# Output products of eight experts with both halves of the second weight in one 512 column operand, the halves added by VectorE, and a new order around them

## The reference

```python
h = gelu(einsum('ecd,edh->ech', buf, w1) + b1[:, None, :])      # 640 x 256 by 256 x 1024
out = einsum('ech,ehd->ecd', h, w2) + b2[:, None, :]            # 640 x 1024 by 1024 x 256
y = einsum('ned,ne->nd', gathered, weights)                     # by gate, summed over experts
x = layernorm(x + y)
```

## Time and profile before

| | |
|---|---|
| median of 3 runs | 974.79 us |
| the profiled execution | 970.69 us, of which the span from first to last instruction is 968.9 us |
| PE busy, share of span | 911.5 us, 94% |
| ACT, DVE, POOL busy | 728.8, 602.7, 455.0 us |
| mean granted TensorE clock | 0.984 |
| experts' part | from 699.9 us to the end at 968.9 us |
| hidden stages (L1518) | 768 products of 320 columns, 116.7 us busy |
| output stages (L1537) | 960 products of 256 columns, 123.8 us busy |

### The profile page before, as it was taken

How to read it: one execution, slowest core, us unless ns; L and a number is a source line. 1 busy time by engine, 2 the same in 40 slices (tenths; PEclk the granted TensorE clock), 3 DMA queues, 4 the chain that set the end, 5 groups by cost and what they waited for, 6 DMA issues and landing times. The chain is left out here.

```text
span 968.9 us, 19742 instructions
## 1 busy us (share of the span) xinstructions
PE 911.5 (94%) x7569; PEld 513.2 (53%) x7569; DVE 602.7 (62%) x1162; ACT 728.8 (75%) x889; POOL 455.0 (47%) x382
## 2 busy tenths in 40 slices
PE   8799999999989999998999999998599999999995
PEld 6333343344333334333433433344599999989994
DVE  5666446547785555787555767347457676667675
ACT  6588878887777888787789789985265678567863
POOL 0265225144355634546464435423525455654574
PEclk9899999999999999999999999999799999999998
DMA  7759442333534335344342327231365434543311
GB/s 219 233 202 353 142 166 70 122 142 132 189 133 159 117 120 186 137 161 136 139 158 100 135 97 239 98 102 35 99 231 164 137 112 135 181 135 108 124 60 61
DMA packets 62201, 139.75 MB, mean 144 GB/s; under 512 B 10242, under 2 KB 31299, under 8 KB 61584
## 3 DMA queue, kind: packets, MB, share of 16 engines
q1 hardware_dynamic: 41040, 74.46, 24.0%
q0 software_dynamic: 21056, 63.93, 18.5%
HBM read 71.43 MB, written 66.54 MB: 142 GB/s over the span
## 5 line engine op out<-in xcount | busy, mean ns | idle before, releaser
L689 ACT ACTIVATE prob<-spsum 128x1024 f32<-128x1024 f32 x512 | 493.1, 1021 | 111.3 <-PE spsum L881 103.3
L905 PE MATMUL opsum<-prob,val 128*17 128x512 f32 x2048 | 271.3, 599 | 1.3 <-DVE oraw L1271 0.4
L881 PE MATMUL spsum<-area_q 32*128 32x512 f32 x1536 | 133.5, 429 | 5.7 <-DMA area_q<-aT 3.3
L881 PE MATMUL spsum<-stacks 32*128 32x512 f32 x1536 | 134.4, 425 | 1.6 <-ACT prob L689 1.0
L881 PEld LDWEIGHTS spsum<-area_q 32*128 32x128 f32 x1536 | 73.1, 185 | 118.5 <-ACT prob L689 63.6
L881 PEld LDWEIGHTS spsum<-stacks 32*128 32x128 f32 x1536 | 73.5, 183 | 115.5 <-ACT prob L689 63.5
L1279 DVE RECIPROCAL oden<-oden 128x256 f32<-128x256 f32 x62 | 108.7, 1753 | 2.1
L574 POOL TENSOR_TENSOR onorm<-oraw,oden 128x512 f32<-128x512 f32 x31 | 41.6, 1343 | 119.5 <-DVE oden L1279 115.1
L519 POOL TENSOR_TENSOR area_s<-emb,area_s 128x1024 fp32r<-128x1024 f32 x28 | 66.5, 2377 | 53.0 <-DVE area_s L1097 53.0
L517 POOL TENSOR_TENSOR square<-raw 128x512 bf16<-128x512 f32 x28 | 53.7, 1918 | 80.3 <-DVE raw L1077 80.2
L905 PEld LDWEIGHTS opsum<-prob,val 128*17 128x17 f32 x2048 | 36.1, 95 | 102.2 <-ACT prob L689 63.9
(11 more groups left out here) (212 smaller groups left out, 1227.1 us busy)
## 6 DMA issues: line engine op xcount, KB each, us to landing
split_scratch<-area_s POOLq DMA_DIRECT2D x60, 512.0 KB, 5.0
area_k<-in_w SPq DMA_DIRECT2D x16, 1024.0 KB, 7.4
stacks<-split_scratch SPq DMA_DIRECT2D x28, 512.0 KB, 5.5
area_q<-split_scratch SPq DMA_DIRECT2D x28, 512.0 KB
dispatched<-blank POOLq DMA_DIRECT2D x1, 5300.0 KB, 25.3
rows<-dispatched SPq DMA_DIRECT2D x7, 662.5 KB
res<-in_x SPq DMA_DIRECT2D x4, 1024.0 KB, 9.3
aT<-onorm SPq DMA_DIRECT2D x124, 32.0 KB
```

Of the source, the lines that this page charges most:

```text
L689: act.activation(prob[u % NPB][:], spsum[u % NSB][:].rearrange("p a n -> p (a n)"), ACT.Exp, scale=HD ** -0.5).then_inc(s_exp, 1)
L881: ins = pe.matmul(spsum[u % NSB][:, j % 2, :], kst[par][rows, a, P * kt:P * (kt + 1)], qst[par][rows, b, cols], start=i == 0, stop=i == 2 ...
L905: ins = pe.matmul(opsum[32 * j:32 * j + HD + 1, :], val[b % 2][:, kt, h0 + j, :], prob[(2 * s + j // 2) % NPB][:, HALF * (j % 2):HALF * (j ...
```

## The change

The order of the three products changes and their form: for each slice m one product of 512 columns takes the high half of the hidden values by both halves of w2 (`high_part`); its result fills the whole bank `yp`, the right half holding the contribution of the low half of w2. One product of 256 columns (`low_part`) adds low by high into the left half. So 16 products replace 24 in a tile, with the same count of columns. `add_own` gets a second DVE instruction that adds the right half into `others`.

PE's order in tiles 0 and 1 changes: the last slice of tile 0 comes behind half of tile 1's high products. On DVE `prepare`, `scale_and_shift` and `add_own` of tiles 0 and 1 go ahead of `turned`, and `remainder` 2 and 3 both go behind the last tile. ACT's `normalise` calls start at tile 0 and are spread over the tiles, `second_half` comes at tile 2. POOL's `store_outputs` and `gather_sums` move accordingly.

```diff
+            def high_part(e, t, first, end):
+                n = ST * e + t
+                if first == 0 and n >= 2:
+                    pe.wait_ge(s_z, n - 1)
+                for m in range(first, end):
+                    if t == 0:
+                        pe.wait_ge(s_hhi, HK * e + m + 1)
+                    pe.matmul(yp[n % 2][:].rearrange("p (s d) -> p s d", s=2),
+                              hids[:, 0, m, P * t:P * (t + 1)], w2s[e % 2][:, :, m, :],
+                              start=m == 0, stop=False)
+            def low_part(e, t, first, end):
+                n = ST * e + t
+                for m in range(first, end):
+                    if t == 0:
+                        pe.wait_ge(s_hid, HK * e + m + 1)
+                    ins = pe.matmul(yp[n % 2][:, 0:DIM], hids[:, 1, m, P * t:P * (t + 1)],
+                                    w2s[e % 2][:, 0, m, :], start=False, stop=m == HK - 1)
+                if end == HK:
+                    ins.then_inc(s_y, 1)
...
-                    if e + 1 < EXPERTS:
-                        for tt in TURNS[t]:
-                            turn(e + 1, tt)
-                    n = ST * e + t
-                    if n >= 2:
-                        pe.wait_ge(s_z, n - 1)
-                    for m in range(HK):
-                        if t == 0:
-                            pe.wait_ge(s_hid, HK * e + m + 1)
-                        for i, (a, b) in enumerate(TERMS):
-                            ins = pe.matmul(yp[n % 2][:, 0:DIM], hids[:, a, m, P * t:P * (t + 1)],
-                                            w2s[e % 2][:, b, m, :], start=m == 0 and i == 0,
-                                            stop=m == HK - 1 and i == 2)
-                    ins.then_inc(s_y, 1)
+                    if e + 1 < EXPERTS and t != 1:
+                        turn(e + 1, t)
+                    if t == 0:
+                        high_part(e, 0, 0, HK - 1)
+                        low_part(e, 0, 0, HK - 1)
+                        if e + 1 < EXPERTS:
+                            turn(e + 1, 1)
+                        high_part(e, 1, 0, HK // 2)
+                        high_part(e, 0, HK - 1, HK)
+                        low_part(e, 0, HK - 1, HK)
+                    else:
+                        high_part(e, t, HK // 2 if t == 1 else 0, HK)
+                        low_part(e, t, 0, HK)
...
                     if e + 1 < EXPERTS:
                         turned_high(e + 1, t)
-                        if t == 1:
+                        if e:
+                            normalise(e - 1, e - 1, ((0,), (1, 2), (), (3,), (4,))[t])
+                        if t == 2:
                             second_half(e + 1)
-                        if e and t >= 2:
-                            normalise(e - 1, e - 1, ((0, 1), (2, 3), (4,))[t - 2])
...
                 dve.wait_ge(s_y, n + 1)
+                link(dve.scalar_tensor_tensor(others[:, t, :], yp[n % 2][:, DIM:2 * DIM], g, others[:, t, :],
+                                              ALU.mult, ALU.add))
                 dve.scalar_tensor_tensor(eo[e % 2][:, t, :], yp[n % 2][:, 0:DIM], g, others[:, t, :],
                                          ALU.mult, ALU.add).then_inc(s_z, 1)
...
-                    if e + 1 < EXPERTS:
-                        for tt in TURNS[t]:
-                            turned(e + 1, tt)
-                        if t:
-                            remainder(e + 1, t - 1)
+                    if e + 1 < EXPERTS and t >= 2:
+                        turned(e + 1, t)
                     prepare(e, t)
...
                     add_own(e, t)
+                    if e + 1 < EXPERTS:
+                        if t < 2:
+                            turned(e + 1, t)
+                        for part in ((), (0,), (1,), (), (2, 3))[t]:
+                            remainder(e + 1, part)
```

On POOL:

```diff
-                    store_outputs(e - 2, 2)
+                    pool.wait_ge(s_h, HK * e + 2)
                     store_outputs(e - 2, 3)
...
-                    pool.wait_ge(s_h, HK * e + 2 + t)
+                    pool.wait_ge(s_h, HK * e + 3 + t)
                     gather_sums(e, t)
...
-                    if e and t >= 2:
-                        store_outputs(e - 1, t - 2)
-            for t in range(2, ST):
+                    if e and t:
+                        store_outputs(e - 1, t - 1)
+            for t in range(ST - 2, ST):
                 store_outputs(LAST - 1, t)
```

More of the change, by code:

```diff
@@ L1397, in experts @@
         block = ctx.enter_context(nc.Block())
-        TURNS = ((0,), (1,), (2,), (3,), (4,))
         @block.sync
```

## The result

The changed kernel takes 961.7 us (median of 4 runs, 961.35 to 962.78) against 974.58 of the kernel before beside it (4 runs, 972.11 to 976.84): a ratio of 0.9873, with an interval of 0.9853 to 0.9893. The gain is 12.9 us where 7.5 was forecast.

A forecast was written before the change was run, and what follows sets the result against it. Bound: the ACT and DVE chain to tile 2 in experts 1 to 6, DVE's queue in expert 7. Terms -9.8 + 1.2 - 1.1 + 2.3 - 0.1 = -7.5 took 974.8 to 967.3 us; range 962.5 to 974.0.

The forecast's parts named there:

- The bound: Experts 1 to 6: the chain through ACT and DVE, not PE, sets tile 2's start, 7.78 us behind the last gelu.
- DVE's order: Experts 1 to 6: tile 2 starts at gelu + 6.15 instead of 7.78, 9.8 us less before late stores.
- the middle that I took for late stores: Experts 2 to 6: 1.2 us given back for late output stores, between ends of 0 and 2.4.
- The store: `add_own(e, 0)` may wait for the last output store, taken to land 3.35 us after issue; 1.2 us back.
- the bounds 0 and 2.4: Lateness of stores in experts 2 to 6: 0 if POOL's moves bring them in time, 2.4 us if nothing changes.
- The products: Where PE sets the pace, 23 tiles: 231.5 ns per 512-column product, 0.05 us saved a tile, 1.1 us in all.
- Rivals C: High products of 512 columns are dearer: at 269 ns each the gain is gone, at 325 ns 992 us; chance 0.10.
- D (131 ns): High products take 131 ns by the skill page's rule, DVE then sets the pace: 961 us; chance 0.03.
- Expert 7: DVE sets the pace there: five more adds cost 2.6 us, 0.3 back for an earlier start, net 2.3 slower.
- late low parts: Sign of being wrong: remainder pieces behind the last tile delay first low parts until gelus and PE wait; no size given.

The follow-up runs named there:

- turned_later: The kernel before with one move on DVE alone, `turned(e + 1, 0)` behind `add_own(e, 0)`; 960.34 us beside 967.19, ratio 0.9914.
- order_only: The changed kernel with two products of 256 columns for each high one and a single add, new order kept; 961.95 us, ratio 0.9867.
- after_pool_old: The changed kernel with POOL's program of before for output stores, gathers and their waits; 962.77 us beside 967.19, ratio 0.9942.

## Why the forecast was too small, and what in it held

**The bound.** That the start of tile 2 was set by the chain through ACT's rounding and DVE's queue is shown: turned_later moves one instruction of it and the 7.78 become 6.25.

**DVE's order.** Forecast was tile 2 at gelu + 6.15. It is at 6.24 to 6.26 where the store is in time, and 6.6 in experts 2, 5 and 6. With the middle that I took for late stores (1.2 us in all) the term was -8.6; it measured -8.1. What is late next isn't the adds but ACT's copy and PE itself. In expert 1, where the last gelu is at 753.92, the timeline of DVE after the change has

```profile
759.42 0.42 DVE L1662 TENSOR_TENSOR xe<-tp,xe 128x256 fp32r<-128x256 f32 x1 [0.20 <-ACT xe L1585]
```

so the second add is done 0.20 us before ACT's copy, and `turned` ends at 5.92. PE's transpositions begin at 6.08, 0.06 us after tile 1. I had PE free at 5.61, counted from a first transposition 0.43 ahead of the gelu; in expert 2 that gelu was a late one, undisturbed it is 0.20, and two tiles with their transpositions take 6.2 to 6.3 us and not 6.0. turned_later and order_only have one add less and the same 6.25, with waits of 0.7 us for ACT's copy. So the second add costs nothing until a store is late.

**The store.** It is issued no earlier than in before (in expert 2 the last gelu is at 783.38 and the store at 785.30, 1.92 behind it, 1.69 before), but took 2.90 us to land, not the 3.35 I had taken or the 3.80 of the earlier trace rows. DVE waited for it in three experts by 0.4 to 0.5 each, 1.3 us in all, and tile 2 came 1.1 us later for it, close to the 1.2. That the middle came out is partly chance: turned_later has a landing of 3.83, and after_pool_old shows what a later store costs, 3.7 us at one place. I gave the moves on POOL the bounds 0 and 2.4; the upper one had left out the clock.

**The products.** Eight high products take 1.87 us, 234 ns each, and eight low ones 0.94, 117 each; the line through the earlier trace rows gave 231.5 for a high one. A tile takes 2.81 us instead of 2.85, so the saving per tile was right, 0.04 against 0.05. 18 tiles gave 0.7. Expert 0 kept its period (30.84 and 30.80), although its tiles gave 0.25: its first gelu comes 3.56 us behind the first product instead of 3.35, as 3.2 us of the stage lay at half the granted clock and not 2.7. Rivals C (269 ns or more) and D (131 ns) are both out. The Trainium skill (TensorE: Matmul & The Clock Gate, Back-to-back issue gap) has N / 2.4 + 2.5 ns for an isolated gap, 216 ns at 512 columns, and about 131 in a stream; this trace has 234, above both.

**Expert 7.** Forecast +2.3, measured +1.1. From the first add (936.37) to the last (950.60) it is 14.2 us where before had 11.2, 3.1 more. The five adds are 2.6 of it, as forecast; the rest is a wait for ACT's ln and exp in front of the second tile's adds (timeline of DVE):

```profile
939.30 0.16 DVE L1345 TENSOR_TENSOR lnt<-lnt 128x1 f32<-128x1 f32 x1 [0.55 <-ACT lnt L1593]
```

The mis-sized term is the start. The store is in time there, so the first add comes at gelu + 4.49 and not + 5.73; I had taken 0.3 of that 1.24. What follows the last add is 0.6 us shorter too, 9.0 instead of 9.5, and one late gelu less gives 0.1. Why the end is shorter isn't shown.

**The step that failed.** The forecast put the hidden stages at nothing, and they measured -4.5 us. It took the hidden stages as unchanged: every term was counted from the last gelu, and the sum has none for the time from first to last gelu. I wrote that the trace of before shows no case in which late low parts hold the gelus, and didn't ask whether anything else held them. Something did, for 4.5 us, and the rows at hand had it: the last gelus of experts 2, 4 and 6 are 64.48 and 63.54 us apart, 32.2 and 31.8 for one expert, while the last two are 31.24 apart. One undisturbed period is 31.1. Nothing in my account explained the odd microseconds, and these are the gain that I missed. Without them the sum would have been -7.5 against -7.8, well within its range.

Shown is that these delays are gone in the trace where one `turned` is moved, that they go in experts 2 to 7 without the output stores, and that they don't go with POOL's two waits. What happens inside isn't settled. The end of PE's last product and the raise of its semaphore lie up to 1.6 us apart by their records, and nothing in the profile says what the raise waited for. No experiment here moves the stores or the gathers by small steps against the gelus, which would be the next one.

## What to carry to other kernels

Before you cost an edit, compare the period of the repeated stage with itself across its repetitions. Where equal work takes 31.1 and 33.4 us, the difference is a cost that a shift in time can remove, or bring, and it belongs in the range. And a wait of TensorE has two prices: its length, and what the clock does behind it. Here 1.3 us in front of tile 2 were never followed by half the clock, and 1.8 us or more were in four of seven places, at 1.5 us each. Of a change with two halves, look for the smallest part that has the gain: here one moved instruction had it, and the new form of the products, beside the new order, made the part 1.6 us longer. And take a trace of the kernel before in every group of runs: without it nothing shows why nearly the same part was worth 7 us beside one group and 13 beside another.

## What the runs showed of the hardware that I had not expected

The raise of a TensorE semaphore is recorded 0.2 to 1.7 us after the end of the product that raises it, where 0.04 us is usual. This held up a gelu 15 times in each of three traces of before, eight times at the same places, and not once in two traces of the changed kernel. In 14 of the 15 places of the first trace GpSimd issued an indirect store or gather in that time.

The granted clock was 0.66 over 5 us after idle times of TensorE of 1.80, 1.81 (expert 3), 2.04 (expert 5) and 2.52 us. It stayed at 1.00 after another of 1.81 (expert 2) and after those of 1.29.

The stores that engines waited for took 2.90, 3.23, 3.80 and 3.83 us to land, for a tile of 128 rows of 256 values.

The kernel without most of its output stores ended 12.1 us behind its last one, twice, instead of 4.4. Why isn't known.
